# Causal mask of the first score pass moved from TensorE's mask products into VectorE's row maxima

## The chip, the cores and the metric

The kernel runs on one core of one Trainium2 chip. The metric is the device time of one launch in microseconds (us).

## The reference

One block of a network on 16 sequences of 512 positions and 256 features. `xn` is the layer-normed input. Two branches read it, and both are added to the input:

```python
x = x + scan_branch(xn) + ffn_branch(xn)

# ffn_branch: causal attention with latent projections, then experts
scores = einsum('bqhd,bkhd->bhqk', qq, kk) * scale          # 16 heads of 16
scores = where(causal, scores, finfo.min)
probs = softmax(scores)
x = x + einsum('bhqk,bkhd->bqhd', probs, v) @ W_o
shared = silu(xt @ Wg_s) * (xt @ Wu_s) @ Wd_s               # shared expert
x = x + shared + combined                                   # 2 of 7 routed experts

# scan_branch: gated state-space scan over 512 steps, 512 channels x 16 states
state = clip(state * dA + x_t * dB); y_t = einsum(state, C_t) + D * x_t
```

The change concerns the causal scores and the shared expert's `silu`.

## The kernel before

The program has three stages, one after another: `build_attn` (attention, shared expert, routing, with the rows scattered to the experts' tables), `build_experts` (routed experts) and the scan.

`build_attn` works in rounds, one for each of the 16 sequences. A list ORDER, written out by hand, names the items of a round, and each engine walks through the same list and does its own part of each item. An item belongs to a sequence that is 3 rounds ahead to 2 behind the round's own (table STAGE), so the stage is a software pipeline. The first rounds lack the later items and the last rounds the earlier ones. The list is built on 62 slots, which hold the second-pass score products ("s2"), their value products ("pv") and most copies of the outputs ("oc"); everything else is laid between them.

Softmax is done in two passes. The first pass ("s1", a sequence ahead of the second) makes the scores only to find each row's maximum: TensorE writes blocks of 128 queries by all keys up to them into a PSUM bank of the ring Y (two banks), and VectorE reduces each row to its negated maximum in `nm`. For each pair of heads there are three items: j = 0 and 1 take one head each, with the 512-key block in one bank and the 384-key and 128-key blocks together in the next; j = 2 takes the 256-key blocks of both heads in one bank. That is 5 banks for a pair of heads and 40 for a round. The maxima are then split in three bf16 parts ("nm"), transposed by TensorE ("nmt") and sent as extra rows of the queries, so that the second pass gets scores less their maxima, which ScalarE puts through the exponential ("f_pt").

The diagonal blocks must be masked. Before the change `hide` does that on TensorE in both passes: a further matmul of an identity with a constant tile, `mask_q` in the first pass and `mask_k` in the second, adds -1e30 above the diagonal, on top of the scores in PSUM. In the first pass it covers 128 columns of the 512-key bank, two blocks of 128 in the bank with 384 and 128, and two in the bank with 256 and 256.

Other names: ring Z holds the banks of all projections; "kq" are the key and query projections with their rotary products on VectorE (`ra`, `rb`); "wo" is the output projection; "g", "u" and "d" are the gate, up and down products of the shared expert. In "g" ScalarE writes tanh of the gate product into `th`, VectorE multiplies into `sg` with (tanh + 1), then with the up product in place, and TensorE reads the same buffer (`hm`) for "d" in the next round but one of the list. `taken` is a semaphore that only counts; its increment gives the wait ahead of it an instruction to stand on.

Of the kernel before, what the change touches and what calls it, by code (L numbers as in the profile page):

```python
# [16 lines left out]
def build_attn(nc, ctx, x_tm, out_tm, info_dram, run_dram, stat_dram, hs, w_ln1, w_ln2, W_kvd, W_qd, W_ka, W_kra, W_krb, W_qa, W_qb, W_vu, W_o,  # L17
# [18 lines left out]
    def sb(name, shape, dt=f32):  # L36
        return ctx.enter_context(nc.sbuf_tensor(name, shape, dt))
# [25 lines left out]
    mask_q = sb("f_mask_q", [P, P], bf16)  # L63
# [59 lines left out]
    th = sb("f_th", [P, NS, SEQ])  # L123
    sg = sb("f_sg", [P, NS, SEQ])
    hm = sg
# [84 lines left out]
    def before_(r):  # L210

        return (r[0], 0) if r[1] else (r[0] - 1, 1)
# [212 lines left out]
    def _(pool):  # L425
# [11 lines left out]
        def masks_and_ones():  # L437
# [3 lines left out]
            fixed(pool.memset(mask_q[:, :], 0.0))  # L441
            fixed(pool.affine_select(out=mask_q[:, :], in_=mask_q[:, :], compare_op=ALU.is_ge, fill=MASKED,
# [93 lines left out]
    def _(act):  # L536
# [12 lines left out]
        def do(kind, i, j, b, r):  # L549
# [54 lines left out]
            if kind == "g":  # L604
                act.wait_ge(*filled(("g", i), r))
                if not isinstance(b, int) or b > 0:
                    act.wait_ge(*used(("g", i), before_(r)))
                act.activation(th[:, i, :], bank_of(("g", i), r)[:, :], ACT.Tanh, scale=0.5).then_inc(th_ready, 1)
# [3 lines left out]
    def _(dve):  # L612
# [4 lines left out]
        def do(kind, i, j, b, r):  # L617
            def row_max(k, out, cols, last=True):
                ins = dve.tensor_reduce(out, cols(full(k, r)), AX.X, ALU.max, negate=True)  # L619
                if last:  # L620
                    ins.then_inc(free_sem(k, r), 1)
# [26 lines left out]
            if kind == "s1":  # L648
                h = 2 * i
                if i == 0 and j == 0:  # L650
                    dve.wait_ge(nm_step, 5 * b)
                if j < 2:
                    row_max(("s1", i, j, 0), nm[:, 3, h + j:h + j + 1], lambda bank: bank[:, :])
                    row_max(("s1", i, j, 1), nm[:, 2, h + j:h + j + 1], lambda bank: bank[:, 0:384], last=False)
                    row_max(("s1", i, j, 1), nm[:, 0, h + j:h + j + 1], lambda bank: bank[:, 384:512])
                else:
                    row_max(("s1", i, j, 0), nm[:, 1, h:h + 2], lambda bank: bank[:, :].rearrange("p (h n) -> p h n", h=2))
# [107 lines left out]
    def _(pe):  # L765
# [57 lines left out]
        def scores(bank, c0, h, qb, p):  # L823

            n = P * (qb + 1)
            pe.matmul(bank[:, c0:c0 + n], qst[p][0:KS, h, qb * P:(qb + 1) * P], kst[p][0:KS, h, 0:n],  # L826
                      start=(c0 == 0), stop=False, skip_group_check=True)
# [35 lines left out]
        def attend(kind, i, j, b, r):  # L863
            p = parity(kind, r)
            if kind == "s1":
                if isinstance(b, int) and b == 0:
                    pe.wait_ge(const_ready, N_CONST)
                h = 2 * i
                if j == 0 and i % 4 == 0:
                    pe.wait_ge(stacked[i // 4], 16 * NSTACK * (b + 1))  # L870
                if j < 2:
                    bank = free(("s1", i, j, 0), r)
                    scores(bank, 0, h + j, 3, p)
                    full(("s1", i, j, 0), r, hide(bank, 384, P, 1, mask_q))
                    bank = free(("s1", i, j, 1), r)
                    scores(bank, 0, h + j, 2, p)
                    scores(bank, 384, h + j, 0, p)
                    full(("s1", i, j, 1), r, hide(bank, 256, P, 2, mask_q))
                else:
                    bank = free(("s1", i, j, 0), r)  # L880
                    scores(bank, 0, h, 1, p)
                    scores(bank, 256, h + 1, 1, p)
                    full(("s1", i, j, 0), r, hide(bank, P, 2 * P, 2, mask_q))
# [1176 lines left out]
```

## Time and profile before

| | |
|---|---|
| median of 3 runs | 4080.77 us (4069.5 to 4081.09) |
| profiled execution, its own time | 4091.09 us |
| its span | 4089.3 us |
| TensorE busy | 3649.6 us (89%) |
| VectorE busy | 2936.9 us (72%) |
| ScalarE busy | 2505.8 us (61%) |
| GpSimd busy | 2193.6 us (54%) |
| mean granted TensorE clock | 0.954 of full |

Busy times are sums over three stages that have different limits, so the table says little of any one of them. PE is TensorE's matmul queue, PEld its weight loads, DVE is VectorE, ACT ScalarE, POOL GpSimd. The span runs from the first to the last instruction of one profiled execution.

### The profile page before, as it was taken

The page shows a single profiled execution, that of the slowest core. Times are in us where ns is not written, and L with a number is a line of the kernel's source. Part 1 is how long each engine was busy: PE and PEld are TensorE (multiplying, and loading weights), DVE is VectorE, ACT ScalarE, POOL GpSimd, SP SyncE. Part 2 cuts the span into 40 slices and gives each one's busy share as a digit, 9 for nine tenths or more (in the row PEclk, how much of TensorE's full clock was granted, in tenths as well). Part 3 has the DMA queues.
Part 4 walks back from the last instruction along what each step waited for, and adds up shares of the span by engine and source line. Part 5 has one row for each costly group of instructions (what it writes and reads, how often), then busy time and mean ns, then how long its engine had stood idle before and what let it go on. Part 6 is the DMA issues. An engine that isn't in the chain of part 4 may idle for free.

```text
span 4089.3 us, 70514 instructions
## 1 busy us (share of the span) xinstructions
PE 3649.6 (89%) x22264; PEld 2745.8 (67%) x22264; DVE 2936.9 (72%) x5456; ACT 2505.8 (61%) x6505; POOL 2193.6 (54%) x1115
## 2 busy tenths in 40 slices
PE   5999999999999659998799999999999999899987
PEld 2455555545554447777588888888888888888776
DVE  3566555565555122222699999999999999999997
ACT  1445444454444213332678788787888878888773
POOL 3244344334442200000487787877878788787774
PEclk8899999999999779999899999999999999999998
DMA  4333342333332157666222122221222222122221
GB/s 113 98 93 113 93 120 88 104 107 112 100 101 79 43 153 209 209 207 194 78 81 98 70 103 83 80 98 64 98 82 91 87 76 98 70 103 83 80 80 39
DMA packets 286369, 417.04 MB, mean 102 GB/s; under 512 B 78261, under 2 KB 250678, under 8 KB 263672
## 3 DMA queue, kind: packets, MB, share of 16 engines
q1 hardware_dynamic: 273048, 381.12, 29.2%
q0 software_dynamic: 12288, 33.57, 2.3%
q8 instruction: 106, 1.74, 0.2%
q10 hardware_dynamic: 864, 0.10, 0.0%
q14 instruction: 63, 0.52, 0.0%
HBM read 330.63 MB, written 83.17 MB: 101 GB/s over the span
## 4 chain that ended last, share of the span: by engine, by line
DVE 36%; issue 11%; PE 3%; ACT 2%; DVEq 1%; POOL 1%; DMA 0%; SPq 0%; ACTq 0%; POOLq 0%
DVE m_S L1760 8%; DVE m_PR L1760 8%; DVE m_S L1752 8%; DVE m_PR L1752 8%; DVE m_ub L1737 1%; ACT m_dA L1649 1%; DVE m_yz L1771 1%; DVE m_x L1721 1%; DVE m_th_x L1729 1%; DVEq L1751 1%; PE m_F L1870 1%; PE m_Y L1908 1%; POOL m_ub L1540 0%; PE m_F L1920 0%; PE m_F L1868 0%
## 5 line engine op out<-in xcount | busy, mean ns | idle before, releaser
L1540 POOL TENSOR_TENSOR m_ub<-m_Bb,m_dtx 128x2048 f32<-128x2048 f32 x254 | 1156.6, 4565 | 284.2 <-PE m_Y L1908 175.9
L1649 ACT ACTIVATE m_dA<-m_dt,m_a_neg 128x128 f32<-128x128 f32 x4096 | 1211.2, 388 | 135.0 <-DVE m_S L1760 134.6
L1908 PE MATMUL m_Y<-m_ub,m_ident 128*128 128x128 f32 x8192 | 956.3, 278 | 67.9 <-DVE m_ub L1737 67.6
L1908 PEld LDWEIGHTS m_Y<-m_ub,m_ident 128*128 128x128 f32 x8192 | 939.5, 194 | 79.2 <-DVE m_ub L1737 78.8
L546 ACT ACTIVATE f_pt<-f_X 128x512 f32<-128x512 f32 (+1 forms) x704 | 374.0, 557 | 512.8 <-PE f_X L843 506.7
L619 DVE TENSOR_REDUCE f_nm<-f_Y 128x1 f32<-128x512 f32 (+3 forms) x896 | 432.0, 531 | 249.4 <-PE f_Y L843 241.8
L1752 DVE SCALAR_TENSOR_TENSOR m_PR<-m_dA,m_S 128x512 f32<-128x512 f32 x512 | 355.8, 695 | 24.7 <-POOL m_ub L1540 6.3
L1752 DVE SCALAR_TENSOR_TENSOR m_S<-m_dA,m_PR 128x512 f32<-128x512 f32 x512 | 354.7, 693 | 12.0
L1760 DVE CUSTOM_DVE_ANT_1 m_S<-m_S,m_ub 128x512 f32<-128x512 f32 x512 | 352.8, 689 | 2.2 <-issue 2.2
L1760 DVE CUSTOM_DVE_ANT_1 m_PR<-m_PR,m_ub 128x512 f32<-128x512 f32 x512 | 352.9, 689 | 0.2 <-DVE m_PR L1752 0.2
L1737 DVE TENSOR_TENSOR m_ub<-m_S,m_Cb 128x512 f32<-128x512 f32 x512 | 349.7, 683 | 0.0
L1737 DVE TENSOR_TENSOR m_ub<-m_PR,m_Cb 128x512 f32<-128x512 f32 x512 | 349.7, 683 | 0.0
L1870 PE MATMUL m_F<-m_xpad,m_cv_diag 128*128 128x256 f32 x1024 | 285.1, 426 | 0.0
L1186 DVE SCALAR_TENSOR_TENSOR e_sg<-e_th,e_G 128x512 f32<-128x512 f32 x70 | 48.1, 688 | 326.9 <-ACT e_th L1130 326.9
L832 PE MATMUL f_X<-f_qst,f_kst 99*128 99x512 bf16 (+3 forms) x1024 | 250.4, 311 | 31.3 <-ACT f_pt L546 19.9
L826 PE MATMUL f_Y<-f_kst,f_qst 96*128 96x512 bf16 (+3 forms) x1024 | 236.0, 315 | 30.6 <-issue 15.8
L1491 POOL MEMSET m_ident<- 128x128 f32 x1 | 0.2, 204 | 472.7 <-POOLq L2037 472.7
L1870 PEld LDWEIGHTS m_F<-m_xpad,m_cv_diag 128*128 128x128 f32 x1024 | 201.4, 207 | 71.7 <-issue 45.5
L1844 PE MATMUL m_F<-m_xnT,m_w_in 128*128 128x256 f32 x1024 | 234.7, 383 | 3.1 <-DMA m_w_in<-L_attn_W_in 2.1
L1844 PEld LDWEIGHTS m_F<-m_xnT,m_w_in 128*128 128x128 f32 x1024 | 192.2, 193 | 28.2 <-DMA m_w_in<-L_attn_W_in 2.5
L510 POOL TENSOR_TENSOR f_yT<-f_yT,f_shares 128x1024 f32<-128x1024 f32 x32 | 75.1, 2348 | 250.2 <-DMA f_shares<-f_shares_dram 250.2
L859 PE MATMUL f_O<-f_pt,f_va 128*32 128x512 f32 (+3 forms) x2048 | 199.9, 464 | 2.7 <-ACT f_pt L546 2.7
(232 smaller groups left out, 6082.8 us busy)
## 6 DMA issues: line engine op xcount, KB each, us to landing
m_Bb<-m_bc_dram SPq DMA_DIRECT2D x64, 1024.0 KB, 4.8
m_Cb<-m_bc_dram SPq DMA_DIRECT2D x64, 1024.0 KB, 6.2
f_parts_dram<-f_parts SPq DMA_DIRECT2D x32, 768.0 KB, 3.7
f_kst<-f_parts_dram SPq DMA_DIRECT2D x192, 128.0 KB, 2.9
f_qst<-f_parts_dram SPq DMA_DIRECT2D x192, 128.0 KB, 3.1
e_rows<-sorted_rows SPq DMA_DIRECT2D x70, 256.0 KB, 2.8
e_wg<-Wg SPq DMA_DIRECT2D x70, 256.0 KB, 2.9
e_wu<-Wu SPq DMA_DIRECT2D x70, 256.0 KB, 4.1
```

Of the source, the lines that this page charges most:

```text
L546: act.activation(out, cols(bank_of(k, r)), func, **kw).then_inc(free_sem(k, r), 1)
L619: ins = dve.tensor_reduce(out, cols(full(k, r)), AX.X, ALU.max, negate=True)
L826: pe.matmul(bank[:, c0:c0 + n], qst[p][0:KS, h, qb * P:(qb + 1) * P], kst[p][0:KS, h, 0:n], start=(c0 == 0), stop=False, skip_group_check= ...
L832: pe.matmul(bank[:, c0:c0 + n], kst[p][:, h, kb * P:(kb + 1) * P], qst[p][:, h, kb * P:SEQ], start=(c0 == 0), stop=False, skip_group_check ...
L1540: pool.tensor_tensor(ub[:, h, i, :, :], Bb[:, s, :, :], dtx[:, m, None, s * SN:(s + 1) * SN].to_broadcast([P, NST, SN]), ALU.mult).then_in ...
L1649: last = act.activation(dA[:, h, i, n, :], dtt[:, par, m, s * SN:(s + 1) * SN], ACT.Exp, scale=a_neg[:, m, n:n + 1])
L1737: return dve.tensor_tensor(ub[:, h, 1:3, :, cols], state[:, :].rearrange("p (i n b) -> p i n b", i=2, n=NST), Cb[:, s, None, :, cols].to_b ...
L1752: dve.scalar_tensor_tensor(new, dA[:, h, :, :, cols].rearrange("p i n b -> p (i n) b"), DA_MIN, old, ALU.max, ALU.mult).then_inc(p_step, 1)
L1760: dve._custom_dve(bass.dve_ops.TENSOR_ADD_SAT, out=new, in0=new, in1=ub[:, h, 0:2, :, cols].rearrange("p i n b -> p (i n) b"), s0=CLIP, s1 ...
L1844: last = pe.matmul(F[(1 + i) % 4][:, m, :], w_in[:, k, blk * P:(blk + 1) * P], xnT[:, k, :], start=(k == 0), stop=(k == KM - 1))
L1870: last = pe.matmul(F[1 + i][:, j, :], cv_diag[:, k * MI + m, :], xpad[:, m, k * BATCH:k * BATCH + CN], start=False, stop=(k == TAPS - 1))
L1908: last = pe.matmul(Y[:, i * SN:(i + 1) * SN], ident[:, :], ub[:, h, 1 + i, n, :], start=False, stop=(n == NST - 1), skip_group_check=True)
```

## The change

The first pass loses its mask products. The last score product into a bank now closes the group and signals VectorE. A tile `causal` of 128 x 512 in bf16 takes the place of `mask_q`: zero, with -1e30 above the diagonal of its last 128 columns. For each block of n keys VectorE runs one `tensor_tensor_reduce` with the last n columns of `causal` in place of the `tensor_reduce`: it adds the mask, multiplies by -1, writes that back into the bank, and gives the minimum as the row's negated maximum. This instruction has one output column, so the item j = 2, once a single reduction with two outputs, takes two. A wait with a `taken` increment stands ahead of the first of each bank. VectorE waits for the constants before its first maxima. The second pass is as before.

Apart from that `th` becomes the same buffer as `sg`. ScalarE then waits, before a tanh, for the "d" product of the list's current round in place of the gate product's release in the round before.

```diff
-    mask_q = sb("f_mask_q", [P, P], bf16)
+    causal = sb("f_causal", [P, SEQ], bf16)
...
-    th = sb("f_th", [P, NS, SEQ])
     sg = sb("f_sg", [P, NS, SEQ])
+    th = sg
...
-            fixed(pool.memset(mask_q[:, :], 0.0))
-            fixed(pool.affine_select(out=mask_q[:, :], in_=mask_q[:, :], compare_op=ALU.is_ge, fill=MASKED,
+            fixed(pool.memset(causal[:, :], 0.0))
+            fixed(pool.affine_select(out=causal[:, SEQ - P:SEQ], in_=causal[:, SEQ - P:SEQ], compare_op=ALU.is_ge, fill=MASKED,
                                      base=0, pattern=[[-1, P]], channel_multiplier=1))
...
                 if not isinstance(b, int) or b > 0:
-                    act.wait_ge(*used(("g", i), before_(r)))
+                    act.wait_ge(*filled(("d", 1), r))
...
-            def row_max(k, out, cols, last=True):
-                ins = dve.tensor_reduce(out, cols(full(k, r)), AX.X, ALU.max, negate=True)
+            def row_max(k, out, c0, n, last=True):
+                if c0 == 0:
+                    dve.wait_ge(*filled(k, r))
+                    dve.sem_inc(taken)
+                cols = bank_of(k, r)[:, c0:c0 + n]
+                ins = dve.tensor_tensor_reduce(out=cols, in0=cols, in1=causal[:, SEQ - n:SEQ], scale=-1.0, scalar=-MASKED,
+                                               op0=ALU.add, op1=ALU.min, accum_out=out)
...
+                if isinstance(b, int) and b == 0:
+                    dve.wait_ge(const_ready, N_CONST)
                 if j < 2:
-                    row_max(("s1", i, j, 0), nm[:, 3, h + j:h + j + 1], lambda bank: bank[:, :])
-                    row_max(("s1", i, j, 1), nm[:, 2, h + j:h + j + 1], lambda bank: bank[:, 0:384], last=False)
-                    row_max(("s1", i, j, 1), nm[:, 0, h + j:h + j + 1], lambda bank: bank[:, 384:512])
+                    row_max(("s1", i, j, 0), nm[:, 3, h + j:h + j + 1], 0, 512)
+                    row_max(("s1", i, j, 1), nm[:, 2, h + j:h + j + 1], 0, 384, last=False)
+                    row_max(("s1", i, j, 1), nm[:, 0, h + j:h + j + 1], 384, 128)
                 else:
-                    row_max(("s1", i, j, 0), nm[:, 1, h:h + 2], lambda bank: bank[:, :].rearrange("p (h n) -> p h n", h=2))
+                    row_max(("s1", i, j, 0), nm[:, 1, h:h + 1], 0, 256, last=False)
+                    row_max(("s1", i, j, 0), nm[:, 1, h + 1:h + 2], 256, 256)
...
-                    scores(bank, 0, h + j, 3, p)
-                    full(("s1", i, j, 0), r, hide(bank, 384, P, 1, mask_q))
+                    full(("s1", i, j, 0), r, scores(bank, 0, h + j, 3, p))
...
-                    scores(bank, 384, h + j, 0, p)
-                    full(("s1", i, j, 1), r, hide(bank, 256, P, 2, mask_q))
+                    full(("s1", i, j, 1), r, scores(bank, 384, h + j, 0, p))
...
-                    scores(bank, 256, h + 1, 1, p)
-                    full(("s1", i, j, 0), r, hide(bank, P, 2 * P, 2, mask_q))
+                    full(("s1", i, j, 0), r, scores(bank, 256, h + 1, 1, p))
```

## Rows read from the trace of the kernel before

**Rows 1.** The page: the chain that ended last, shares by line.
```profile
DVE m_S L1760 8%; DVE m_PR L1760 8%; DVE m_S L1752 8%; DVE m_PR L1752 8%; DVE m_ub L1737 1%; ACT m_dA L1649 1%; DVE m_yz L1771 1%; DVE m_x L1721 1%; DVE m_th_x L1729 1%; DVEq L1751 1%; PE m_F L1870 1%; PE m_Y L1908 1%; POOL m_ub L1540 0%; PE m_F L1920 0%; PE m_F L1868 0%
```

**Rows 2.** Windows: us, busy PE, PEld, DVE, ACT, POOL; clock, DMA, GB/s.
```profile
744.00:911.30 167.30, 160.34 (x969) 85.67 (x969) 98.28 (x242) 79.67 (x151) 67.07 (x66) 0.96 0.36 103
911.30:1078.00 166.70, 159.75 (x982) 85.87 (x984) 99.10 (x251) 81.13 (x154) 67.10 (x66) 0.98 0.35 104
...
59.80:107.30 47.50, 41.30 (x145) 16.86 (x146) 33.75 (x71) 8.27 (x11) 13.88 (x10) 0.72 0.39 122
107.30:166.50 59.20, 55.89 (x342) 26.41 (x343) 35.14 (x82) 31.18 (x57) 17.19 (x18) 0.93 0.30 89
```

**Rows 3.** Waits of TensorE, 200 to 1,300 us: total, times, longest.
```profile
PE f_X L832 <- ACT f_pt L546: 13.3, 40, 0.5
...
PE f_Y L826 <- DVE f_nm L619: 8.4, 16, 1.2
PE f_Z L889 <- DVE f_sg L752: 7.3, 13, 1.0
```

**Rows 4.** Groups by form, up to 1,350 us: busy, mean ns, idle before.
```profile
L619 DVE TENSOR_REDUCE f_nm<-f_Y 128x1 f32<-128x512 f32 x256 | 175.5, 686 | 231.0 <-PE f_Y L843 224.9 <-issue 5.8
...
L843 PE MATMUL f_Y<-f_mask_q,f_identb 128*128 128x256 bf16 x384 | 109.5, 285 | 0.0
...
L619 DVE TENSOR_REDUCE f_nm<-f_Y 128x1 f32<-128x128 f32 x256 | 71.9, 281 | 0.0
...
L843 PE MATMUL f_Y<-f_mask_q,f_identb 128*128 128x128 bf16 x256 | 58.8, 230 | 0.0
```

**Rows 5.** Timeline at 710 us: start, duration, instruction, count.
```profile
710.14 0.22 PE L843 MATMUL f_Y<-f_mask_q,f_identb 128*128 128x128 bf16 x1
...
710.20 0.38 PE L826 MATMUL f_Y<-f_kst,f_qst 96*128 96x384 bf16 x2
...
710.41 0.27 PE L843 MATMUL f_Y<-f_mask_q,f_identb 128*128 128x256 bf16 x1
...
710.53 0.38 PE L832 MATMUL f_X<-f_qst,f_kst 99*128 99x256 bf16 x2
```

**Rows 6.** Timeline of VectorE: two smallest instructions, and the scan's custom one.
```profile
842.35 0.17 DVE L662 COPY f_mvx<-f_sc 128x4 f32<-128x4 f32 x1
842.43 0.17 DVE L663 COPY f_mvx<-f_sc 128x4 f32<-128x4 f32 x1
...
2300.72 0.69 DVE L1760 CUSTOM_DVE_ANT_1 m_PR<-m_PR,m_ub 128x512 f32<-128x512 f32 x1
2301.32 0.41 DVE L1771 TENSOR_TENSOR m_yz<-m_Y,m_zs 128x256 f32<-128x256 f32 x1
```

**Rows 7.** Timeline of VectorE in a dense stretch of a steady round.
```profile
889.11 1.32 DVE L619 TENSOR_REDUCE f_nm<-f_Y 128x1 f32<-128x512 f32 x3
890.34 0.69 DVE L645 TENSOR_TENSOR f_ra<-f_Z,f_rope 128x512 f32<-128x512 f32 x1
890.94 0.69 DVE L647 TENSOR_TENSOR f_rb<-f_Z,f_rope 128x512 f32<-128x512 f32 x1
891.54 1.35 DVE L619 TENSOR_REDUCE f_nm<-f_Y 128x1 f32<-128x512 f32 x3
```

**Rows 8.** Timeline of TensorE in the same stretch.
```profile
892.28 0.39 PE L826 MATMUL f_Y<-f_kst,f_qst 96*128 96x256 bf16 x2 [0.52 <-DVE f_nm L619]
```

**Rows 9.** Timelines: down and gate product on VectorE; the constants; the first scores.
```profile
848.78 0.69 DVE L760 SCALAR_TENSOR_TENSOR f_xs<-f_Z,f_xs 128x512 f32<-128x512 f32 x1 [0.88 <-PE f_Z L956]
...
907.70 0.69 DVE L752 SCALAR_TENSOR_TENSOR f_sg<-f_th,f_Z 128x512 f32<-128x512 f32 x1 [2.34 <-ACT f_th L608]
...
24.58 0.90 POOL L456 MEMSET f_va<- 128x960 f32 x1
36.49 1.27 POOL L492 TENSOR_TENSOR f_kq<-f_ra,f_rb 128x512 f32<-128x512 f32 x1 [11.02 <-issue]
...
59.85 0.59 PE L826 MATMUL f_Y<-f_kst,f_qst 96*128 96x512 bf16 x1 [15.76 <-issue]
```

More of the change, by code:

```diff
@@ L825, in scores @@
             n = P * (qb + 1)
-            pe.matmul(bank[:, c0:c0 + n], qst[p][0:KS, h, qb * P:(qb + 1) * P], kst[p][0:KS, h, 0:n],
-                      start=(c0 == 0), stop=False, skip_group_check=True)
+            return pe.matmul(bank[:, c0:c0 + n], qst[p][0:KS, h, qb * P:(qb + 1) * P], kst[p][0:KS, h, 0:n],
+                             start=(c0 == 0), stop=True, skip_group_check=True)
         def scores_t(bank, c0, h, kb, p):
```

## The prediction

> **What bounds the kernel now.** I began with the page's 40 slices and its chain of waits. They split the kernel in three: the fused attention and shared-expert stage up to about 1,430 us, the routed experts to about 2,000 us, and a scan in which VectorE sets the end (the chain's heaviest lines are all its own) [rows 1]. The diff touches the first stage only, so I read the windows of that stage. The reader should see there that two steady rounds take 166.7 to 167.3 us, so one takes about 83.5, and that TensorE is busy for 80.0 of them, VectorE for 49.3, ScalarE for 40.2 and GpSimd for 33.5 [rows 2]. TensorE paces this stage. The chain followed back from the end never reaches it, because the three stages run one after another: whatever a round loses here is lost from the total.
>
> Next the list of waits, for TensorE alone, over 1,100 us (about 13 rounds). The matmul queue stood still 40 times for ScalarE's probabilities (13.3 us), 16 times for VectorE's row maxima (8.4 us) and 13 times for the product of the shared expert ahead of the transposes of the maxima (7.3 us) [rows 3]. Each is short: TensorE is nearly always late itself, and it is late by its own work.
>
> **What goes from TensorE.** A round loses 40 mask products: 16 of 128 columns (full-length rows), 16 of 256 (the bank of 384 and 128 columns) and 8 of 256 (the two blocks of 256). Their listed durations, 230 and 285 ns [rows 4], are mostly pipeline depth, so I price them by the distance from one start to the next. The 128-column product starts at 710.14 and the next matmul at 710.20: 0.06 us. The 256-column one starts at 710.41 and the next at 710.53: 0.12, and 0.105 is what its columns would take at the rate of the two score products in front of it (512 columns in 0.21); I take 0.11 [rows 5]. A round then saves 16 x 0.06 + 24 x 0.11 = 3.6 us. All 16 rounds with first-pass scores hold 57.6 us. The identity's weight loads go too; they lie under the running product and I cost them at nothing. The granted clock is 0.96 to 0.98 of full in these windows [rows 2], which would lift the saving by some 2 us; I leave it out.
>
> The Trainium skill ("TensorE: Matmul & The Clock Gate", Back-to-back issue gap) says that in a stream of weight loads and matmuls a 128-column pair costs about 81 ns. By it the 16 short products would give 1.3 us a round instead of 0.96, or about 5 us more over the stage. The trace shows 0.06 us and is what the sum uses.
>
> **What VectorE gets.** Seven reductions of a group of heads become eight fused ones: the 2 x 256 reduction is split. The columns stay the same, 20,480 a round. No instruction in the trace does what the new one does: read a bank of PSUM and a bf16 mask, write back into the same bank, and put out a minimum beside it. Its parts are bounded by the nearest rows.
>
> The stream itself: a 512-column reduction takes 686 ns, one of 128 takes 281 ns [rows 4]. The scan stage's instruction of the same custom kind takes 0.69 us for 512 columns, and the next starts 0.60 us after it [rows 6]; the reductions follow one another at the same distance, three of them (1,024 columns) within 1.23 us [rows 7]. So I price the stream at no more than now. The split costs one more start-up, 0.60 less the 0.53 that 512 columns take by the slope between the two reductions (686 - 281 over 384 columns is 1.05 ns each, so 0.54), 0.06 us, 8 times a round: 0.5 us.
>
> The second output: at least nothing (it rides along), at most 0.17 us, the whole duration of the smallest VectorE instruction. Two such instructions start 0.08 us apart [rows 6], and that is the value I take, since the result is a 128 x 1 column. 64 x 0.08 = 5.1 us a round. The separate wait and semaphore increment before each bank I put at nothing: the scan's custom instruction has the same pair in front of it and the queue in front runs on. VectorE's load rises from 49.3 to about 55 us of 80. It does not become the bound as a whole; the cover is its idle time waiting for scores.
>
> The Trainium skill ("VectorE: DVE Perf Modes", Two Vector instructions with no wait between them) counts an operation that also writes out its accumulator as two instructions. By that rule the read is a further small instruction; with the smallest start-to-start distance the sum is the one above, with nothing for it the forecast would be some 10 us lower. No row of this trace shows such a pair.
>
> **Where VectorE's extra time comes through.** In one stretch of each round it has no slack: from 889.11 to 892.89 it runs reductions, both rope products and reductions again without a gap [rows 7], and TensorE waits 0.52 us for the bank that the second group's first reduction frees [rows 8]. Four fused instructions come before that release: 4 x 0.08 = 0.32 us later. TensorE would arrive 0.34 us earlier, the masks of the two items ahead of it being gone, and that saving is only waited away. The queue behind it holds another four and a split: 0.4 us. So 1.1 us a round is not gained. The 16 waits in 13 rounds [rows 3] say that this happens about once a round. ScalarE: 3 waits a round of TensorE on the exponentials; an earlier arrival by one mask product is lost at each: 0.3 us. For smaller stalls elsewhere, 0.1. The wait for the shared expert's product before the maxima are transposed [rows 3] has no first-pass scores behind the last arrival from TensorE, so it stays as it is.
>
> Net: 3.6 - 1.5 = 2.1 us a round. It counts in the 14 rounds that TensorE paces (the window from 107.3 to 166.5 us, with TensorE busy 55.9 of 59.2, among them): 29 us. In the first, from 59.8 to 107.3 us, there are no second-pass scores, VectorE is busy 33.8 of 47.5 [rows 2], and earlier filling and slower emptying about cancel; I count 1 us. Sum 30 us.
>
> **The other edits.** The tanh now overwrites the product's buffer. ScalarE waits for the down-projection of the batch before, which VectorE has already drained at 848.78 us, while the gate's product comes at 907.70 [rows 9]: 58 us of cover, cost nothing. If that cover were gone, ScalarE's exponentials behind it would wait, and with them TensorE. The fused gate operation keeps its operand count. VectorE waits for the constants before the first maxima: GpSimd has written them by 25.5 us, the first-pass scores start at 59.85. The mask tile is four times as wide to clear, a few tenths of a microsecond, and GpSimd's next work begins at 36.49 after 11 us of idle time [rows 9]: nothing. No DMA is added, removed or moved.
>
> The profiled execution took 4091.09 us around a span of 4089.3; the sum gives 4061 for it. It was 10.3 us above the median of 4080.77. From the median the forecast is 4051 us, 0.7% less. Its own range is 4041 (the second output free: 5.1 us less on VectorE, 0.7 us a round less lost, 14 rounds) to 4065 (0.17 us each: 1 us a round more lost).
>
> **The rivals.**
> Nearly the whole gain comes through: TensorE's few waits are not made longer, because VectorE's queue catches up in its idle time and the second output costs nothing. Then 50 to 57 us go: 4027. For it: TensorE is busy 80.0 of 83.5 us. Against: the waits of [rows 3] exist and lie right behind removed products. Chance 0.22, from 4023 to 4040.
>
> The saving is swallowed. TensorE's pace is only apparent, and the round is held by the hand-over to ScalarE and VectorE: each of the removed products covers an exponential or a reduction. Then the round stays at 83 us, and the time at 4069 to 4093, say 4078. For it: 40 + 16 + 13 waits; against: together they are 29 of 1,100 us. Chance 0.17.
>
> Slower: the write back into the bank being read. VectorE never writes PSUM in this trace. If reading and writing one bank takes a second cycle for each column, the 20,480 columns cost another 21 us a round. VectorE would then carry 49.3 + 21 + 6 = 76 us of a round of 80, with its waits for rope, gate and output products in between. TensorE would wait at most of the 40 banks; with 0.1 to 0.2 us at each the round grows by 4 to 8 less the 3.6 saved, plus VectorE's own excess in the dense stretches, in all some 6 us, and the first round by half of 21: 15 x 6 + 10 = 100 us, 4180 us. The same sign comes from any price above about 0.2 us an instruction: the tight stretches hold some 16 of them, and 16 x 0.2 eats 3.2 of the 3.6 us. Chance 0.13, nearly all of it slower than 4093.
>
> **How the numbers follow.** About 0.3%, 12 us, is what a measurement of this kernel can tell from no change. The forecast has 0.48 (4041 to 4068), the full gain 0.22, swallowed 0.17, slower 0.13. Faster: 0.70, same 0.17, slower 0.13. The range leaves out most of the slower case and the far end of the full gain: 4030 to 4088.
>
> **What would show it.** Right: no mask product of the first pass left; the fused instruction at about 0.69 us for 512 columns and three of them within 1.5 us; a pair of rounds at about 163 us; TensorE's wait for the maxima at 892 grown to over 1 us. Wrong: an instruction of over a microsecond for 512 columns (then slower), a read of the second output of over 0.17 us, VectorE busy over 60 us a round, or TensorE's waits for ScalarE doubled with the round unchanged.

## The result, and the profile after

The changed kernel takes 4056.03 us (median of 9 runs, 4053.53 to 4061.23) against 4081.09 for the kernel before (9 runs, 4066.42 to 4091.88): a ratio of 0.9943, 95% interval 0.9928 to 0.9957, 25 us less. The prediction said 4051. The number was nearly right, and the reason was for the larger part wrong, as the last runs below show: that the two agree is luck.

The profiled execution took 4060.19 us. Its page, the span and the busy times:

```profile
span 4058.4 us, 71021 instructions
...
PE 3605.3 (89%) x21624; PEld 2691.9 (66%) x21624; DVE 3002.6 (74%) x6608; ACT 2503.4 (62%) x6505; POOL 2195.5 (54%) x1115
```

TensorE lost 44 us of busy time and VectorE gained 66. The span is 30.9 us shorter than that of before (4089.3), more than the 25 between the medians, because the profiled execution of before lay 10.0 us above its median and this one 4.2. All but 0.3 us of it arises in the first stage: the last split of the maxima lies at 1277.53 us, where before it lay at 1308.15.

The mask products of the first pass are gone. What VectorE does in their place, as groups by form up to 1,350 us, answers to the reductions in [rows 4]:

```profile
L623 DVE CUSTOM_DVE_ANT_0 f_Y<-f_Y,f_causal 128x512 f32<-128x512 f32 x256 | 179.0, 699 | 190.4 <-PE f_Y L834 169.9 <-issue 18.5
...
L623 DVE DVE_READ_ACCUMULATOR2_ANT f_nm<- 128x1 f32 x1024 | 143.8, 140 | 1.6 <-issue 1.6
...
L623 DVE CUSTOM_DVE_ANT_0 f_Y<-f_Y,f_causal 128x128 f32<-128x128 f32 x256 | 84.6, 330 | 0.0
```

The fused instruction lasts 699 ns for 512 columns, where the reduction lasted 686, and 330 for 128 columns, where it lasted 281. The minimum is put out by an instruction of its own, listed with 140 ns. How much of that counts is seen only in a timeline, here of VectorE in the dense stretch that answers to [rows 7]:

```profile
870.06 0.70 DVE L623 CUSTOM_DVE_ANT_0 f_Y<-f_Y,f_causal 128x512 f32<-128x512 f32 x1
870.68 0.14 DVE L623 DVE_READ_ACCUMULATOR2_ANT f_nm<- 128x1 f32 x1
870.68 0.60 DVE L623 CUSTOM_DVE_ANT_0 f_Y<-f_Y,f_causal 128x384 f32<-128x384 f32 x1
871.19 0.14 DVE L623 DVE_READ_ACCUMULATOR2_ANT f_nm<- 128x1 f32 x1
871.19 0.33 DVE L623 CUSTOM_DVE_ANT_0 f_Y<-f_Y,f_causal 128x128 f32<-128x128 f32 x1
871.44 0.14 DVE L623 DVE_READ_ACCUMULATOR2_ANT f_nm<- 128x1 f32 x1
871.44 0.69 DVE L650 TENSOR_TENSOR f_ra<-f_Z,f_rope 128x512 f32<-128x512 f32 x1
```

The next instruction starts together with the read. From 870.06 to 871.44 three blocks take 1.38 us, where three reductions took 1.23 in [rows 7]: 0.05 us each, not the 0.14 of the list and not the 0.08 that was forecast.

TensorE in the same stretch, answering to [rows 8]:

```profile
873.45 0.39 PE L834 MATMUL f_Y<-f_kst,f_qst 96*128 96x256 bf16 x2 [0.86 <-DVE f_nm L623]
...
875.00 0.39 PE L834 MATMUL f_Y<-f_kst,f_qst 96*128 96x384 bf16 x2 [0.40 <-DVE f_nm L623]
...
878.63 0.39 PE L834 MATMUL f_Y<-f_kst,f_qst 96*128 96x256 bf16 x2 [0.34 <-DVE f_nm L623]
```

The wait of 0.52 us has become one of 0.86, with two more behind it. The list of TensorE's waits, 200 to 1,300 us (total, times, longest), shows it for the whole stage and answers to [rows 3]:

```profile
PE f_Y L834 <- DVE f_nm L623: 25.6, 48, 1.6
PE f_X L840 <- ACT f_pt L546: 14.9, 45, 0.5
PE f_Z L894 <- DVE f_sg L760: 8.1, 14, 0.8
```

The wait for a bank of ring Y went from 8.4 us in 16 places to 25.6 in 48. Two pairs of rounds, each from one split of the maxima to the next but one, in the windows' columns of [rows 2]:

```profile
571.69:732.32 160.63, 153.30 (x890) 77.91 (x890) 104.47 (x387) 79.68 (x151) 67.13 (x66) 0.97 0.36 108
651.31:812.11 160.80, 153.49 (x890) 77.94 (x890) 104.88 (x387) 79.71 (x151) 67.13 (x66) 0.97 0.36 106
```

A pair takes 160.6 to 160.8 us, where it took 166.7 to 167.3 [rows 2]. That is 3.2 us a round, more than the forecast 2.1, although TensorE's waits for VectorE are longer by 1.3 us a round. Something else must have gone, and it is an entry that the prediction passed by. In the same list of waits of the kernel before stands

```profile
PE f_X L832 <- issue: 8.5, 4, 2.3
```

and there is no such line after the change. In the timeline of TensorE before, two of the four are

```profile
758.32 0.61 PE L832 MATMUL f_X<-f_qst,f_kst 99*128 99x512 bf16 x1 [2.30 <-issue]
...
925.87 0.60 PE L832 MATMUL f_X<-f_qst,f_kst 99*128 99x512 bf16 x1 [2.29 <-issue]
```

They lie one trip of the hardware loop apart; the other two, at 423.41 and 590.77, last 1.89 and 2.06 us. `run` unrolls the first five and the last six rounds and puts the ten between them in a loop of five trips with two rounds each; the stall is at its back edge. The trace of before has rounds with and without it, in the windows' columns:

```profile
575.89:662.09 86.20, 81.80 (x485) 43.73 (x485) 47.51 (x123) 40.02 (x76) 33.54 (x33) 0.94 0.34 99
662.09:743.20 81.11, 78.79 (x485) 42.05 (x485) 48.03 (x122) 39.90 (x76) 33.55 (x33) 0.98 0.37 107
```

The round with the edge takes 5.1 us more than the one without. TensorE stands still for 2.1 us of it, and the granted clock is lower behind it, 0.94 against 0.98 over the round, which shows as 3.0 us more of busy time for the same 485 products. Windows right behind the standstill that ends at 590.77 show where:

```profile
590.00:598.00 8.00, 7.23 (x27) 4.69 (x28) 2.08 (x5) 1.79 (x3) 1.19 (x4) 0.57 0.52 136
598.00:606.00 8.00, 8.00 (x65) 5.01 (x62) 6.24 (x15) 6.45 (x13) 5.49 (x8) 1.00 0.55 168
```

After 2.06 us without work TensorE runs for some 7 us at a granted clock of 0.5 to 0.6, the lower of its two levels (1.2 GHz) for most of it, and then at the full 2.4 GHz again. Four such rounds, at 5.1 us each, are 20 us.

### The profile page after: what moved, and what is told of

Its sections match the earlier page's. It is cut to its first block, busy times and chain, and to the rows that moved or that the text cites. A ratio compares the mean times of both kernels' runs of the same rounds, so it can differ in the third digit from the quotient of the medians.

```text
span 4058.4 us, 71021 instructions
## 1 busy us (share of the span) xinstructions
PE 3605.3 (89%) x21624; PEld 2691.9 (66%) x21624; DVE 3002.6 (74%) x6608; ACT 2503.4 (62%) x6505; POOL 2195.5 (54%) x1115
## 4 chain that ended last, share of the span: by engine, by line
DVE 37%; issue 11%; PE 1%; POOL 1%; DVEq 1%; ACT 1%; DMA 0%; SPq 0%; POOLq 0%; ACTq 0%
DVE m_S L1765 8%; DVE m_PR L1765 8%; DVE m_S L1757 8%; DVE m_PR L1757 8%; DVE m_ub L1742 2%; DVE m_yz L1776 1%; DVE m_x L1726 1%; POOL m_ub L1545 1%; DVEq L1756 1%; DVE m_th_x L1734 1%; ACT m_dA L1654 0%; PE m_Y L1913 0%; PE m_F L1849 0%; PE m_F L1875 0%; PE m_F L1925 0%
## 5 line engine op out<-in xcount | busy, mean ns | idle before, releaser
L623 DVE CUSTOM_DVE_ANT_0 f_Y<-f_Y,f_causal 128x512 f32<-128x512 f32 (+3 forms) x1024 | 476.1, 518 | 202.6 <-PE f_Y L834 179.4
L834 PEld LDWEIGHTS f_Y<-f_kst,f_qst 96*128 96x128 bf16 x1024 | 87.9, 102 | 197.5 <-DVE f_nm L623 87.7
```

The costliest lines, as they stand in the source:

```text
L623: ins = dve.tensor_tensor_reduce(out=cols, in0=cols, in1=causal[:, SEQ - n:SEQ], scale=-1.0, scalar=-MASKED, op0=ALU.add, op1=ALU.min, acc ...
L834: return pe.matmul(bank[:, c0:c0 + n], qst[p][0:KS, h, qb * P:(qb + 1) * P], kst[p][0:KS, h, 0:n], start=(c0 == 0), stop=True, skip_group_ ...
```

## The experiments

The first kernels ask about the terms of the prediction, the last five about the loop. For each kernel the distance from the third to the fifteenth split of the maxima, 12 rounds, is given beside the time. It leaves out the ends of the stage, and it comes from one profiled execution. It is 989.5 us before and 953.3 after.

### The other edit alone

```diff
 # the kernel before, with:
+    th = sg
...
-                    act.wait_ge(*used(("g", i), before_(r)))
+                    act.wait_ge(*filled(("d", 1), r))
```

> The kernel before with the tanh written into the product's buffer and the new wait, nothing else. My theory: nothing, 4081 us within 5, because the wait is met some 50 us early in each round. Rival (part of the gain comes from the tanh's wait): 4070 or less. The wait for the down product in place of the release costs something: 4086 or more.

4079.84 us, ratio to before 0.9994 (0.998 to 1.0008), 12 rounds in 986.5. The edit costs and brings nothing by itself.

### No mask in the first pass

```diff
 # the changed kernel, with:
-                ins = dve.tensor_tensor_reduce(out=cols, in0=cols, in1=causal[:, SEQ - n:SEQ], ...)
+                ins = dve.tensor_reduce(out, cols, AX.X, ALU.max, negate=True)
...
-                read(("s2", i, j), probs(i, j), ..., ACT.Exp)
+                read(("s2", i, j), probs(i, j), ..., ACT.Exp, scale=0.05)
```

It leaves the first pass's mask out, so the maxima are over all keys, and it scales the exponent.

> The changed kernel with the first pass left unmasked and the old plain reductions on VectorE; the exponential's argument is scaled by 0.05 so that no sum underflows. It leaves out the first pass's mask and changes the softmax. So TensorE has lost its mask products and VectorE pays nothing. My theory: the longer instructions on VectorE give back about 1.2 us of each of 14 rounds, so this is 15 to 20 us below the changed kernel, about 4038 us. Rival (VectorE's price is hidden, the rest is lost to ScalarE and to hand-overs): 4056, as the changed kernel.

4042.18 us, ratio 0.9898 (0.9881 to 0.9915): the mask on VectorE costs the changed kernel about 14 us (4056.03 less 4042.18, or 0.45% of 4,081 by the ratios: 18). The waits of TensorE in this kernel:

```profile
PE f_Y L834 <- DVE f_nm L625: 21.5, 47, 1.5
PE f_X L840 <- ACT f_pt L546: 16.6, 46, 0.5
```

With VectorE doing the same reductions as before, TensorE waits for them 21.5 us in 47 places. TensorE's own earlier arrival at a ring of two banks is therefore enough for 13.1 of the 17.2 us by which the wait grew, with 4.1 for VectorE's longer work on top. How the 17.2 divide depends on the order in which they are added, as the next kernel shows. Its 12 rounds take 950.7 us, only 2.6 less than the changed kernel's. The larger part of the price lies ahead of them: from the first score product to the third split it takes 184.9 us, the changed kernel 191.8 and the kernel before 186.3. Windows of before, changed kernel and this one, one line from each:

```profile
59.85:246.14 186.29, 172.78 (x941) 81.30 (x941) 107.75 (x242) 78.67 (x141) 56.74 (x53) 0.87 0.34 100
```
```profile
62.70:254.48 191.78, 171.04 (x821) 73.24 (x821) 120.03 (x458) 78.24 (x141) 56.84 (x53) 0.82 0.33 98
```
```profile
61.87:246.74 184.87, 165.17 (x821) 71.16 (x821) 108.03 (x242) 78.34 (x141) 56.75 (x53) 0.85 0.34 101
```

In the rounds that fill the pipeline the fused instructions cost 6.9 us, part of it through the granted clock (0.82 against 0.85). Of the 15.0 us between the two spans another 4.7 lie behind the fifteenth split; nothing here says why.

### Both masks

```diff
 # the changed kernel, with:
+    mask_q = causal[:, SEQ - P:SEQ]
...
-                    full(("s1", i, j, 0), r, scores(bank, 0, h + j, 3, p))
+                    scores(bank, 0, h + j, 3, p)
+                    full(("s1", i, j, 0), r, hide(bank, 384, P, 1, mask_q))
...
```

> The changed kernel with TensorE's mask products of the first pass put back, so that the mask is added twice: VectorE pays its price and TensorE gains nothing. My theory: 9 to 15 us above the kernel before, 4090 to 4096 us, since 0.05 us for each of the output reads and the split show only in the dense stretch. Rival (the instruction on VectorE costs nothing on the path): 4081. A second rival, that TensorE's saved time is worth more than 3.6 us a round and VectorE's price too: over 4100.

4101.49 us, ratio 1.004 (1.0025 to 1.0056); 12 rounds in 992.9. So the fused instructions on top of the kernel before cost 16 us, the same as the 14 to 18 by the other route. TensorE's waits for the maxima:

```profile
PE f_Y L835 <- DVE f_nm L624: 19.8, 45, 0.8
```

Here VectorE's longer work alone, with TensorE no earlier than before, raises them from 8.4 to 19.8 us, by 11.4. So either change alone makes most of the new waiting, and together they make less than their sum. The stall at the edge is there as before: `issue`, 7.2 us, 4 times. The step from both_masks to the changed kernel, 40 us by the ratios and 45 by the medians, therefore holds the mask products (57.6 us in the prediction) and the edge together.

### The masked scores to another buffer

```diff
 # the changed kernel, with:
+    side = sb("f_side", [P, 2, SEQ], bf16)
...
-                ins = dve.tensor_tensor_reduce(out=cols, in0=cols, ...
+                ins = dve.tensor_tensor_reduce(out=side[:, place(k, r)[0], c0:c0 + n], in0=cols, ...
```

> The changed kernel with the fused instruction's main output sent to a bf16 side buffer in SBUF in place of the bank it reads. If the write back into the bank costs nothing (my theory): 699 ns for 512 columns as before and 4056 us within 4. If it costs part of the 13 ns by which 512 columns became longer than the plain reduction: 686 ns and 2 to 5 us less. If it cost more in contention with TensorE's writes: 4045 or less.

4050.43 us, ratio 0.9911 (0.9889 to 0.9933). By form, to set against the rows of the changed kernel above:

```profile
L624 DVE CUSTOM_DVE_ANT_0 f_side<-f_Y,f_causal 128x512 bf16<-128x512 f32 x256 | 176.2, 688 | 213.3 <-PE f_Y L835 190.2 <-issue 21.0
...
L624 DVE DVE_READ_ACCUMULATOR2_ANT f_nm<- 128x1 f32 x1024 | 85.1, 83 | 1.7 <-issue 1.7
L624 DVE CUSTOM_DVE_ANT_0 f_side<-f_Y,f_causal 128x128 bf16<-128x128 f32 x256 | 73.2, 286 | 0.0
```

688 ns against 699 for 512 columns, 286 against 330 for 128. Writing an fp32 result back into the bank costs 11 to 44 ns an instruction over writing bf16 to SBUF, nothing like another 1.05 ns a column. The interval of the ratio overlaps that of the changed kernel (0.9928 to 0.9957), so a gain over it is likely but not shown.

### A longer VectorE queue

```diff
 # the changed kernel, with, ahead of each fused instruction:
+                dve.tensor_tensor(side[:, place(k, r)[0], int(c0 > 0), :], rope[:, 0, 0:P], rope[:, 1, 0:P], ALU.add)
```

> The changed kernel with one more VectorE instruction (a 128 x 128 addition in SBUF, about 0.2 us start to start) ahead of each of the 64 fused ones of a round. It asks what VectorE's price is worth on the path. The prediction said that 16 instructions of a round stand in dense stretches and that a price of 0.2 us eats the gain: 4056 + 15 x 3.2 = 4104 us, in any case above 4085. Rival (VectorE's idle time absorbs it, 62 us busy of 80): under 4070.

4186.12 us, ratio 1.0253 (1.0233 to 1.0272). VectorE's timeline:

```profile
905.15 0.29 DVE L623 TENSOR_TENSOR f_side<-f_rope 128x128 f32<-128x128 f32 x1
905.35 0.29 DVE L625 CUSTOM_DVE_ANT_0 f_Y<-f_Y,f_causal 128x128 f32<-128x128 f32 x1
```

The added instruction costs 0.20 us from start to start. With it TensorE waits for ring Y 80.0 us in 116 places. Against the changed kernel, 0.20 us more on each of 1,024 instructions costs 130 us, so about 0.6 of what VectorE gets comes through. The prediction let a price of 0.2 us eat 3.2 us a round; it eats some 8.

### Two rotary products earlier, with and without the side buffer

```diff
 # the changed kernel (reorder), in ORDER:
-                           (33, "kq", 1, 2), (33, "kq", 1, 3),
+                           (28, "kq", 1, 2), (30, "kq", 1, 3),
 # the kernel of the side buffer (early_side), in ORDER:
+                           (23, "kq", 1, 2), (24, "kq", 1, 3),
```

> The changed kernel with the two rope products of slot 33 moved to slots 28 and 30, out of the stretch in which TensorE waits 0.86 + 0.40 + 0.34 us for the maxima. If this stretch is where the price comes through: 1 us a round less, about 4042 us. If the waits only move to other places: 4056. If GpSimd's sum of the rope products now holds up its chain before the residual sum: 4060 or more.

> A version meant to beat both: the fused instruction writes to a bf16 side buffer in SBUF, and the two rope products of slot 33 stand at slots 23 and 24, ahead of the output projection with its statistics. The last attempt put them between those and made a new wait of 1.59 us. If the dense stretch is what is left: 1.35 us of waits a round less, 4035 us. If the waits only move: 4048 to 4052, as with the side buffer alone. If the key sums wait for GpSimd's other work: over 4060.

4080.13 us, ratio 0.9995 (0.9982 to 1.0007), and 4077.87, ratio 0.9983 (0.9973 to 0.9994): both are slower than the kernels they were made from, by 24 and 27 us. TensorE's waits for ring Y rose, to 35.1 us in the one (from 25.6) and 32.3 in the other (from 23.6). That is not half of it: over the 12 rounds, 17.8 us longer in the first (971.1 against 953.3), TensorE is busy 10.8 us more for the same 5,340 products (919.6 against 908.8), at a granted clock of 0.97 against 0.98. In the first a new stall stands at 879.45:

```profile
879.45 0.39 PE L834 MATMUL f_Y<-f_kst,f_qst 96*128 96x512 bf16 x1 [1.59 <-DVE f_nm L623]
```

The dense stretch was not removed but moved to where VectorE also adds the output projection.

### Small products for the stall

In the changed kernel each bank gets a product of 8 columns behind its scores, at the place where the mask product stood. It adds zeros. `tiny_masks` has 40 a round, `tiny_some` only the 16 behind the banks of 384 and 128 columns.

```diff
+        def tiny(bank):
+            return pe.matmul(bank[:, 0:8], identb[:, :], causal[:, 0:8], start=False, stop=True, skip_group_check=True)
...
-                    full(("s1", i, j, 1), r, scores(bank, 384, h + j, 0, p))
+                    scores(bank, 384, h + j, 0, p)
+                    full(("s1", i, j, 1), r, tiny(bank))
```

> The changed kernel with TensorE's 40 removed products of a round put back as products of 8 columns that add zeros: all its instructions are there again, nearly none of their columns. Theory found in the traces: part of the gain is that a loop trip of two rounds has fewer TensorE instructions, so that the stop of 2.3 us at the loop's start (4 times, with a stretch of low clock behind it, about 5 us each) is gone. Then the four stops come back, for about 20 us, with 10 to 20 us for the products themselves: 4085 to 4095 us. Rival (only columns count, the missing stops are chance): no stops and 4056 to 4068 us.

> As the last, with 16 of the 40 products of 8 columns in a round (one behind each bank of 384 and 128 columns). A loop trip then has 64 TensorE instructions more than the changed kernel and 96 fewer than the kernel before. If it is a matter of a fixed store that the trip must fit into, near 2,048 instructions by the count of the records, this one still fits: no stop of 2 us, and 4060 to 4068 us. If each added instruction costs alike, it has part of the stops, and stands in the middle between the changed kernel and the last.

4072.69 us where 4085 to 4095 was expected, ratio 0.9972 (0.9961 to 0.9983), and 4064.82, ratio 0.9955 (0.994 to 0.9969). The waits of TensorE in `tiny_masks`:

```profile
PE f_Y L834 <- DVE f_nm L623: 24.4, 48, 1.5
...
PE f_X L840 <- issue: 8.3, 4, 2.3
```

and in `tiny_some`:

```profile
PE f_X L840 <- issue: 3.6, 4, 1.0
```

The stall is back, four times, 1.9 to 2.3 us in the timeline of the one and 0.7 to 1.0 in that of the other. The expectation for `tiny_some` held two readings against each other, a store of some 2,048 instructions that the trip fits into or not, and a price that grows with the number; the fixed store would have given no stall, and the stall came. In `tiny_masks` the rounds alternate again between 83.5 us with the edge and 78.6 without. TensorE's busy time of one trip is as in the changed kernel (153.4 us for 970 products against 153.3 for 890), but over the 12 rounds it is 8.2 us more (917.0 against 908.8); how much of that is the small products' own work and how much the clock behind the edge stays open. In the trace a trip has 970 + 970 products and weight loads and 167 records of TensorE's sequencer (register operations, waits and increments, the branch) in `tiny_masks`, 2,107 in all; 2,011 in `tiny_some`; 1,947 in the changed kernel; 2,107 before. In time the two kernels lie 17 and 9 us above the changed one by the medians, while their 12 rounds take 966.2 and 956.6 us, 12.9 and 3.3 more than its 953.3.

### The loop of TensorE written out

```diff
 # the kernel before (before_unrolled) and the changed one (after_unrolled), in run:
-        with nc.Fori(1, BATCH // 2 - 2, engines=[eng.engine], hint_back_edge=True) as g:
-            rnd((g, 0))
-            rnd((g, 1))
+        if eng is nc.tensor:
+            for n in range(1, BATCH // 2 - 2):
+                rnd((n, 0))
+                rnd((n, 1))
+        else:
+            with nc.Fori(1, BATCH // 2 - 2, engines=[eng.engine], hint_back_edge=True) as g:
+                rnd((g, 0))
+                rnd((g, 1))
```

> The kernel before, with TensorE's loop of five trips written out as ten rounds; the other engines keep their loops, and TensorE does the same products in the same order. Theory A: TensorE's stall of 2.3 us at each of the four back edges, and the slower round around it (86.1 us against 81.1), come from the jump back in a loop whose trip has about 2107 of TensorE's instructions. Without a back edge they go: no issue wait on the product behind the edge, no round above 83 us between the fourth and the thirteenth, 15 to 20 us less than before, 4065 to 4070 us. Theory B: the stall belongs to the work at that place of a trip (the first second-pass product of the next round), and the time is that of before within 0.3%.

> The changed kernel with TensorE's loop written out in the same way. Its trip has about 1946 of TensorE's instructions and its trace shows no stall at the edges. Theory A (the change's removal of 160 instructions a trip freed it of the stall already): nothing more to be had, the time of the changed kernel within 0.2%, 4050 to 4060 us, so that the difference between the two unrolled kernels is only 5 to 12 us of the 25. Theory B (written-out rounds help or hurt both kernels alike, whatever the trip's length): this kernel moves as much as the other does.

before_unrolled: 4059.01 us (9 runs; before 4084.96 beside it), ratio 0.9939 (0.9921 to 0.9957). The kernel before, with every mask product in place, comes within 3 us of the changed one, which the intervals do not tell apart. That is 26 us less, where 15 to 20 were expected. after_unrolled: 4054.2 us, ratio 0.9932 (0.9909 to 0.9956). So theory A held for both: much from the one, nothing that can be told from zero from the other. The waits of TensorE in before_unrolled have no `issue` line for the second-pass products, and those for VectorE are the old ones:

```profile
PE f_X L837 <- ACT f_pt L551: 14.7, 43, 0.5
PE f_Y L831 <- DVE f_nm L624: 8.4, 16, 1.2
```

Its window over the round that took 86.20 us before:

```profile
565.52:646.58 81.06, 78.82 (x485) 42.05 (x485) 47.65 (x122) 39.84 (x76) 33.60 (x33) 0.98 0.36 106
```

Behind the same place, from 580 to 595, it has TensorE busy for all of the 15 us at a granted clock of 1.00. And the 12 rounds, of before_unrolled:

```profile
244.42:1209.37 964.95, 937.88 (x5820) 502.46 (x5820) 581.95 (x1454) 478.32 (x901) 403.27 (x396) 0.99 0.36 107
```

of after_unrolled:

```profile
248.52:1196.63 948.11, 904.87 (x5340) 461.56 (x5340) 631.05 (x2318) 477.18 (x901) 402.49 (x396) 0.99 0.37 109
```

Against the kernel before (989.5 us, TensorE busy 952.5) the written-out loop takes 24.6 us from the 12 rounds. Of these 14.7 are busy time of the same 5,820 products, the clock's share, and 9.9 are standstill, 8.5 of it the `issue` waits.

Without the edge the change takes 16.8 us from the 12 rounds, 1.4 a round, while TensorE's busy time falls by 33.0, or 2.75 a round. About half of the saving is waited away. By the medians the two unrolled kernels differ by 4.8 us, and by the ratios by 0.07% with an interval of about 0.3% (12 us) either way. The profiled execution of the one was 6.0 us above its median, that of the other 4.4 below, which is most of why the traces differ by more.

### Increments in the loop alone

```diff
 # the changed kernel, at the end of each first-pass item:
+                if not isinstance(r[0], int):
+                    for _ in range(4 if j < 2 else 2):
+                        pe.sem_inc(taken)
```

> The changed kernel, with 160 increments of the semaphore that only counts added to TensorE's queue in each trip of the loop and none outside: about 2106 instructions a trip, with no matmul, weight load or work for another engine more. Theory A: the stall returns at all four edges with about 2 us each, as with the 80 small products a trip, and the time rises by 8 to 15 us to 4064 to 4071. Theory B (it was the added products that cost, not their number in the loop): no issue wait at the edge, the time of the changed kernel within 0.1%.

4070.28 us (10 runs), ratio 0.9965 (0.9951 to 0.9979): 14 us more than the changed kernel by the medians, 9 by the ratios, with no product more. The stall came back at every edge, but in another shape than expected. TensorE at one of them:

```profile
585.35 0.39 PE L840 MATMUL f_X<-f_qst,f_kst 99*128 99x512 bf16 x1 [0.66 <-issue]
...
587.87 1.89 PE L964 MATMUL f_Z<-f_wd,f_sg 128*128 128x256 f32 x8 [0.94 <-issue]
```

0.5 to 0.8 us at the first product and 0.8 to 1.2 at the next group, together 1.5 to 1.8, or 6.5 us at the four edges. Unlike before, the clock does not fall there (1.00 from 584 to 594). And the increments cost more away from the edges than at them:

```profile
PE f_X L840 <- issue: 8.6, 24, 0.8
...
PE f_O L867 <- issue: 4.1, 16, 0.3
```

Only 4 of the 24, with 2.6 us, stand at an edge; the other 20 and the 16 of the second line make 10.1 us. So this run bears out that a stall at the edge comes back with the number of instructions in a trip, but its 9 to 14 us are not the price of that stall.

## Why the prediction was right, and where it was wrong

**The time** was 4056 where 4051 was forecast, inside the range. The sum behind it was not right: it put all 30 us on a shorter path through the rounds. The number fits because a cost that the sum does not hold, the back edge, went away together with the mask products. The runs put about 20 to 26 us on the back edge of TensorE's loop (26 by before_unrolled, 20 by 86.2 against 81.1 us for a round, four times, in the trace of before). What the traded work brings by itself is 4.8 us by the medians, not told from zero, and 15.2 by the spans of the two unrolled traces.

**What bounds the kernel now** is the step that failed. It read TensorE's waits [rows 3] for ACT, DVE and the product, and left the `issue` line of 8.5 us, 4 times, 2.3 the longest, unread, though its longest was nearly twice the longest of the waits named (1.2). It also priced the steady round as 83.5 us, the mean of two kinds. Nor did any rival hold that fewer instructions could matter for their number.

**What goes from TensorE.** 3.6 us a round was forecast. The busy time of a pair fell from 160.0 to 153.4 us, 3.3 a round, and by 2.75 a round between the unrolled kernels; the rest of the 3.3 goes with the lower clock behind the edge, which makes the same products longer. The prices of 0.06 and 0.11 us by start-to-start distance were somewhat high, or the removed products lay partly under other work. That part stays open.

**What VectorE gets.** Forecast 0.08 us for the second output and 0.06 for each split, 5.6 a round. Measured 0.05 an instruction, and VectorE's busy time of a round rose from 49.3 to 52.3 us, 3.0. The step had the right form: the read is an instruction, its listed 140 ns are no price, and its start-to-start distance is. The Trainium skill ("VectorE: DVE Perf Modes", Two Vector instructions with no wait between them) counts an operation that writes out its accumulator as two instructions; the trace agrees, with 1,024 reads of 140 ns, of which 0.05 us count, here together with the write into the bank.

**Where the extra time comes through.** The dense stretch was the right place: the wait at that bank grew from 0.52 to 0.86, by 0.34 us, half of the 0.66 forecast (0.32 for VectorE's lateness and 0.34 for TensorE's earliness), and two more of 0.40 and 0.34 stand behind it, where 0.4 in all was forecast. The sum, 1.08, is the forecast 1.1, but it came out so by two errors that cancel. The loss was 1.35 us a round where 1.5 was forecast, by the unrolled traces (2.75 less 1.4). The prediction added the two causes; no_mask and both_masks show that either alone makes 13.1 or 11.4 of the 17.2 us of new waiting.

**The first round** was to cancel. Until the third split of the maxima the changed kernel loses 5.5 us against before (191.8 against 186.3), and 6.9 against no_mask. The prediction counted a gain there: 1 us for the first round and 2.1 for each of the next two. **The other edits** cost nothing, as forecast (th_only).

**The rivals.** The full gain needed TensorE's waits not to grow, and they tripled. Slower by a write into the bank being read: 11 ns more for 512 columns settles it against. Swallowed: of the traded work alone, this rival may be the nearest to the truth, since without the edge the change is worth 0.07% with an interval on both sides of zero. Its mechanism (the removed products covered an exponential or a reduction) holds for about half of the saving. The price from which the sign turns was put too high: 0.20 us more an instruction cost 130 us.

```profile
q8 instruction: 56, 0.92, 0.4%
```

A trip takes 10 packets before and 8 to 10 in the changed kernel, so neither trip is kept from one time to the next, and the shorter one is not free of the stall because it fits. What differs is when the first packet of the edge starts: 0.9 to 1.5 us behind the start of the branch before (587.54 for 586.63), between 0.35 ahead and 0.23 behind in tiny_some, 0.2 to 0.6 ahead in counts_in_loop, and 1.9 us or more ahead in the changed kernel (580.53 for a branch at 582.43). By and large, the later it starts, the longer the branch lasts. That the branch waits for this transfer is the reading that fits all of it; no run moved the transfer by itself. The Trainium skill ("Runtime: NRT & Kernel Launch", Instruction fetch mechanics) says that TensorE's instruction memory holds 2048 instructions, is refilled in blocks of 256, and that a taken branch to a target outside the window waits for the fetch. The trace agrees with the blocks and with a branch that waits; it does not bear out 2048 as a size that a trip has to stay under, since 2,011 stalls and 1,947 is fetched anew. Why the transfer starts earlier in the shorter trips stays open, and three sizes of trip are too few to say where the stall begins.

## What to carry to other kernels

Read every line of the bounding engine's waits, "issue" too: here a wait that came once a trip at the back edge was a cost of the loop, and a round's length should be read with the edge and without it before a mean is used. When a change removes many instructions from a loop, try first the same kernel with that engine's loop written out; here a few lines brought 26 us, all that a trade of 640 matrix products against 1,024 longer vector instructions brought. And where an engine hands over through two banks, price a saving by the pair and not by the engine: here about half of what was taken from TensorE was waited away for VectorE.

## What the runs showed of the hardware that was not expected

- A back edge of TensorE's loop cost 1.6 to 2.3 us of standstill with 2,107 records a trip (before, both_masks, tiny_masks), 0.7 to 1.0 with 2,011 and none with 1,947. The branch itself is recorded with 3.0 to 3.9, 2.2 to 2.5 and 0.3 to 0.5 us, and with 0.08 where it is not taken. The round around it was 5 us longer (86.2 against 81.1, and 83.5 against 78.6).
- After the 2.06 us of standstill at 590.77 TensorE ran some 7 us at about half of its clock (0.57 from 590 to 598); over 12 rounds more of the edges' cost was slower products (14.7 us) than standstill (9.9).
- A stall comes back with 160 bare semaphore increments a trip as well, 1.5 to 1.8 us in two pieces at each edge; the increments cost another 10.1 us away from the edges.
- A read of the accumulator is listed with 140 ns (83 ns when the main output goes to SBUF), and the next instruction starts with it; block for block it and the in-place output cost 0.05 us.
- Writing the masked scores back into their bank in fp32 costs 11 ns at 512 columns and 44 at 128 over a bf16 output in SBUF; 0.05 us an instruction on VectorE turned into 14 to 18 us of the kernel's time.
